# Mixture-of-experts tail of a language-model tower: results scattered into rows of their own and summed per batch, instead of accumulated by the DMA

## What is computed

```
h = tok(x)                              # per token: 6-qubit circuit on 36 angles -> 6 numbers -> 192 features
h = h + attention(layernorm(h))         # single head, width 192, per batch
h = h + moe(layernorm(h))               # 8 experts, top 2, gelu MLP 192 -> 384 -> 192
def moe(x):
    scores = x @ Wg;  s, idx = top_k(scores, 2);  p = softmax(s)
    y_e = gelu(x @ W1[e] + b1[e]) @ W2[e] + b2[e]
    return p[0] * y[idx[0]] + p[1] * y[idx[1]]
```

## Time and profile before

| | us |
|---|---|
| median of 3 runs | 389.87 (388.54 to 391.79) |
| profiled execution: span from first to last instruction | 338.6 |
| time of that execution outside the span | not given by the page; against the median 51.3 |
| POOL busy | 250.2 |
| PE busy | 240.9 |
| DVE busy | 177.6 |
| ACT busy | 95.2 |

### The profile page before, as it was taken

The page is one execution under the profiler, slowest core; times in us unless marked ns, Lnnn a source line. Parts: engine busy times, 40 slices in busy tenths (PEclk is TensorE's granted clock), DMA queues, the critical chain, the costliest instruction groups (busy, mean ns, idle before and its releaser), DMA issues. The chain is left out here.

```text
span 338.6 us, 6221 instructions
## 1 busy us (share of the span) xinstructions
PE 240.9 (71%) x1585; PEld 162.0 (48%) x1585; DVE 177.6 (52%) x698; ACT 95.2 (28%) x223; POOL 250.2 (74%) x283
## 2 busy tenths in 40 slices
PE   0831973668478989768654899999999587999500
PEld 0621641223243445444421678777777365877400
DVE  5758997488998866684699322232222122122200
ACT  1002001354324144634233323332432132133000
POOL 5778979309968777766777388888883888888673
PEclk9999995558955556965555599999999799699955
DMA  6710019900000001111123146656461556564510
GB/s 191 201 13 11 0 45 400 382 5 2 2 0 9 12 13 60 63 57 60 59 70 103 22 54 69 64 62 67 53 69 18 60 62 65 61 69 50 59 10 0
DMA packets 28141, 22.61 MB, mean 67 GB/s; under 512 B 15434, under 2 KB 25546, under 8 KB 27787
## 3 DMA queue, kind: packets, MB, share of 16 engines
q0 software_dynamic: 13296, 7.95, 21.1%
q1 hardware_dynamic: 14524, 14.23, 13.0%
q10 hardware_dynamic: 288, 0.03, 0.1%
HBM read 7.25 MB, written 15.63 MB: 68 GB/s over the span
## 5 line engine op out<-in xcount | busy, mean ns | idle before, releaser
L709 POOL DMA_INDIRECT out<-up x71 | 110.3, 1554 | 33.1 <-issue 13.9
L1972 PE MATMUL bank_b<-down,up 128*128 x426 | 91.2, 354 | 5.0 <-DVE up L1473 1.0
L1972 PEld LDWEIGHTS bank_b<-down,up 128*128 128x128 f32 x426 | 72.9, 200 | 22.6 <-issue 18.8
L1473 DVE TENSOR_SCALAR up<-bank_b,up 128x192 f32<-128x192 f32 x71 | 29.6, 418 | 97.5 <-PE bank_b L1972 84.9
L657 POOL DMA_INDIRECT routed<-rows,slot x64 | 61.9, 968 | 23.9 <-issue 18.0
L472 POOL DMA_INDIRECT theta_all<-angles,ids x32 | 32.4, 1012 | 10.9 <-issue 9.0
L1651 ACT ACTIVATE up<-bank_a 128x384 f32<-128x384 f32 x71 | 31.3, 497 | 3.4 <-PE bank_a L1962 2.9
L1775 PE MATMUL bank_b<-queries_t,keys_t 32*128 32x512 f32 x64 | 26.1, 900 | 6.9 <-ACT keys_t L1499 3.4
L1782 PE MATMUL bank_a<-keys_t,wt 32*128 32x512 f32 x64 | 27.6, 949 | 3.8 <-DVE nmax L1133 2.1
L1663 ACT COPY up<-bank_c 128x384 f32<-128x384 f32 x18 | 8.6, 478 | 61.8 <-PE bank_c L1951 58.7
L1133 DVE TENSOR_REDUCE nmax<-bank_a 128x2 f32<-128x1024 f32 x16 | 19.5, 1219 | 11.5 <-PE bank_a L1782 11.3
(11 more groups left out here) (420 smaller groups left out, 369.4 us busy)
## 6 DMA issues: line engine op xcount, KB each, us to landing
routed<-pad_rows SPq DMA_DIRECT2D x8, 528.0 KB, 5.7
out<-hres SPq DMA_DIRECT2D x8, 384.0 KB, 2.4
down<-down_w SPq DMA_DIRECT2D x1, 2304.0 KB, 11.9
up<-up_w SPq DMA_DIRECT2D x1, 1536.0 KB
out<-up POOLq DMA_INDIRECT x71, 3.5
up<-routed SPq DMA_DIRECT2D x69, 16.0 KB
routed<-rows,slot POOLq DMA_INDIRECT x64
up<-up_w SPq DMA_DIRECT2D x1, 780.0 KB
```

The costliest lines, as they stand in the source:

```text
L709: pool.indirect_dma_start(out=out_rows, out_offset=bass.IndirectOffsetOnAxis(xb[:, m // STEP % RING, m % STEP, DEST:DEST + 1].bitcast(I32) ...
L1473: dve.tensor_scalar(y[:, m % RESULTS, :], bank_b[:, m % 2, 0:D], xb[:, m // STEP % RING, m % STEP, SHARE:SHARE + 1], None, ALU.mult).then_ ...
L1972: mm = pe.matmul(bank_b[:, m % 2, 0:D], hid[:, m % STEP, c * P:(c + 1) * P], down[:, bass.ds(first + c * D, D)], start=(c == 0), stop=(c = ...
```

## The change

- GpSimd scatters the results without add, into a DRAM tensor `results` of 8192 rows, one for each token and choice (`DEST` now counts to 2 x TOKENS). The waits on shared blocks, their arithmetic and the early stores of `hres` are gone. The bounds check stays.
- Each batch's two result rows per token are read back (`load_results`) and VectorE adds both to `hres` (`add_results`), then the batch is stored. Batches 0 to 5 are summed inside the loop at blocks fixed in `SUM_AT`, 6 and 7 after it. SyncE reads batch b back when the blocks that can hold its rows have landed.
- The order of the blocks no longer goes by expert alone. The first EARLY = 25 are whole blocks of the first four batches, worked out by `early_table` on VectorE once these are routed, ahead of batch 4's `variance2`. The rest come in groups by batch (what four batches leave whole, then what batches 4, 5, 6, 7 complete), worked out by `late_table`, spread over partitions by one matmul (`late_columns`) and written by `late_numbers`. Within a group they go by expert. 24 blocks are loaded without waiting for the last four batches' rows; the first 16 as soon as four batches are scattered.
- `pick_up` and its copy for steps 0 and 1, and the first `block_transpose`, move into the last attention iterations; ScalarE's GELU table is loaded ahead of the last `a2t_copy`.
- The readback of the last batch waits until the last block with real rows has landed (`need`); blocks after it are padding.

```diff
     RING = 4
-    SEEN = BATCHES - 2
     RESULTS = 8
+    EARLY_BATCHES = CHUNK_BATCHES[0]
+    EARLY = 2 * EARLY_BATCHES * SEQ // P - (E - 1)
+    EARLY_STEPS = EARLY // STEP
+    LATE = BLOCKS - EARLY
+    GROUPS = 2 + BATCHES - EARLY_BATCHES
...
+    results = nc.dram_tensor("results", (2 * TOKENS, D), F32, kind="Internal").ap()
...
+    results_view = results.rearrange("(k b p j) d -> b p k (j d)", k=2, b=BATCHES, j=TILES)
...
+        def whole_after(b):
+
+            return 2 * SEQ * (max(b + 1, EARLY_BATCHES)) // P + E - 2
+
+        def picked_in(s):
+
+            return bank_b[:, s, 0:HID] if s < 2 else bank_c[:, 0:HID]
+
+        SUM_AT = (46, 48, 53, 55, 59, 62)
+        STORE_AT = (45, 47, 51, 53, 57, 60)
...
+            def load_block(m):
+                row = sp.value_load(t_i[0:1, 0, m:m + 1], min_val=0, max_val=ROWS - P)
                 sp.dma_start(xb[:, m // STEP % RING, m % STEP, :], routed[bass.ds(row, P), :]
                              ).then_inc(block_in[m // STEP % RING], 16)
...
+            def load_results(b):
+                sp.dma_start(results_in[b % 2], results_view[b]).then_inc(results_back[b % 2], 16)
+
+            def store(b):
+                sp.wait_ge(summed, b + 1)
+                sp.dma_start(out_view[b], hres[:, b, :]).then_inc(out_done, 16)
+
             sp.wait_ge(table_done, 1)
-            first_rows = [block_row(m) for m in range(0, STEP, 2)]
-            sp.wait_ge(scattered, 16 * (2 * TILES * SEEN - 1))
-            rows_written(0)
-            sp.sem_inc(first_ready, 1)
-            for m, row in zip(range(0, STEP, 2), first_rows):
-                load_block(m, row)
-            for r in range(1, RING):
-                rows_written(r)
-                for m in blocks_of(r):
-                    load_block(m, block_row(m))
-            sp.wait_ge(scattered_last, 16 + 16 * 2 * TILES * (BATCHES - SEEN))
-            for m in range(BLOCKS):
+            sp.wait_ge(scattered_early, 16 * 2 * TILES * EARLY_BATCHES)
+            for m in range(RING * STEP):
+                load_block(m)
+            for m in range(LEAST - 1):
                 sp.wait_ge(added[m % RESULTS], 16 * (m // RESULTS) + 16)
-                sp.sem_inc(landed, 1)
-                if m + RING * STEP < BLOCKS:
-                    load_block(m + RING * STEP, block_row(m + RING * STEP))
-            sp.wait_ge(h2_out, 16 * BATCHES)
+                following = m + RING * STEP
+                if following == EARLY_STEPS * STEP:
+                    sp.wait_ge(table_done, 2)
+                    sp.wait_ge(scattered_late, 16 * 2 * TILES * (BATCHES - EARLY_BATCHES))
+                if following < BLOCKS:
+                    load_block(following)
+                if m == whole_after(0):
+                    load_results(0)
+                    load_results(1)
+                for b in range(BATCHES - 2):
+                    if m == STORE_AT[b]:
+                        store(b)
+                        if b < 3:
+                            load_results(b + 2)
+                for b in (5, 6):
+                    if m == whole_after(b):
+                        load_results(b)
+            last = sp.value_load(need[0:1, 0:1], min_val=1, max_val=BLOCKS - LEAST + 1)
+            sp.wait_ge(landed, last)
+            hold(sp)
+            load_results(BATCHES - 1)
+            store(BATCHES - 2)
+            store(BATCHES - 1)
+            sp.wait_ge(out_done, 16 * BATCHES)
...
-            pool.wait_ge(h2_out, 16 * BATCHES)
-            pool.wait_ge(order_done, 1)
             for m in range(BLOCKS):
-                last_shared = pool.value_load(t_i[0:1, 1, m:m + 1], min_val=1, max_val=BLOCKS + 1)
                 pool.wait_ge(y_done, m + 1)
-                pool.wait_ge(landed, last_shared)
-                hold(pool)
                 pool.indirect_dma_start(
-                    out=out_rows, out_offset=bass.IndirectOffsetOnAxis(
+                    out=results, out_offset=bass.IndirectOffsetOnAxis(
                         xb[:, m // STEP % RING, m % STEP, DEST:DEST + 1].bitcast(I32), 0),
-                    in_=y[:, m % RESULTS, :], in_offset=None, bounds_check=TOKENS - 1,
-                    oob_is_err=False, compute_op=ALU.add).then_inc(added[m % RESULTS], 16)
+                    in_=y[:, m % RESULTS, :], in_offset=None, bounds_check=2 * TOKENS - 1,
+                    oob_is_err=False).then_inc(added[m % RESULTS], 16)
...
+            def early_table():
+
+                step(dve.tensor_scalar(full_i[:, 1, :], full_i[:, 0, :], 7, None, ALU.arith_shift_right))
+                join()
+                step(dve.tensor_copy(full[:, :], full_i[:, 1, :]))
+                step(dve.tensor_copy(cum[:, 0, :], full_i[:, 1, :]))
...
+                step(dve.tensor_scalar(skip[:, :], full[:, :], -float(P), float(REGION), ALU.mult, ALU.add))
+                c = prefix(cum, E, (1, 2, 4))
+                step(dve.tensor_tensor(ge[:, :, :], blk[:, 0:EARLY].unsqueeze(1).to_broadcast([P, E - 1, EARLY]),
+                                       cum[:, c, 0:E - 1].unsqueeze(2).to_broadcast([P, E - 1, EARLY]), ALU.is_ge))
+                join()
+                step(dve.tensor_reduce(t_exp[:, :], ge.rearrange("p e m -> p m e"), AX.X, ALU.add))
+                step(dve.tensor_tensor(ge_w[:, :, :], ge, skip[:, 0:E - 1].unsqueeze(2).to_broadcast([P, E - 1, EARLY]),
                                        ALU.mult))
...
+                join()
+                step(dve.tensor_reduce(t_skip[:, :], ge_w.rearrange("p e m -> p m e"), AX.X, ALU.add))
+                step(dve.tensor_scalar(t_own[:, 0:EARLY, 0], t_exp[:, :], own[:, 0:1], None, ALU.is_equal))
+                step(dve.tensor_scalar(t_i[:, 1, 0:EARLY], t_exp[:, :], float(HC * D), None, ALU.mult))
+                join()
+                dve.scalar_tensor_tensor(t_i[:, 0, 0:EARLY], blk[:, 0:EARLY], float(P), t_skip[:, :], ALU.mult, ALU.add
+                                         ).then_inc(table_done, 1)
...
+            def late_table():
+
+                counted = bank_c[:, COUNT_AT:COUNT_AT + (GROUPS - 1) * E].rearrange("p (g e) -> p g e", e=E)
+                step(dve.tensor_scalar(count_i[:, 1:GROUPS], counted, float(P - 1), None, ALU.add))
+                step(dve.tensor_copy(count_i[:, 0], counted[:, 0]))
...
+                h = prefix(run_end, RUNS, (1, 2, 4, 8, 16, 32))
+                end = run_end[:, h, :]
+                step(dve.tensor_tensor(run_n[:, :], run_n[:, :], end, ALU.subtract))
+                step(dve.tensor_scalar(run_ge[:, :], end[:, 0:RUNS - 1], pos[:, 0:1], None, ALU.is_le))
+                step(dve.tensor_scalar(need[:, :], end[:, RUNS - 1:RUNS], -float(LEAST - 1), None, ALU.add))
...
+                step(dve.tensor_reduce(late[:, 0:2], run_w[:, :, :], AX.X, ALU.add))
+                join()
+                step(dve.tensor_tensor(late[:, 2:3], late[:, 1:2], pos[:, :], ALU.add))
+                step(dve.tensor_scalar(late_diag[:, 0, :], ident[:, 0:LATE], late[:, 0:1], None, ALU.mult))
+                join()
+                dve.tensor_scalar(late_diag[:, 1, :], ident[:, 0:LATE], late[:, 2:3], None, ALU.mult
+                                  ).then_inc(late_ready, 1)
...
+            def late_numbers():
+
+                dve.wait_ge(late_spread, 1)
+                step(dve.tensor_scalar(t_own[:, EARLY:BLOCKS, 0], bank_c[:, 0:LATE], own[:, 0:1], None,
+                                       ALU.is_equal))
+                step(dve.tensor_scalar(t_i[:, 1, EARLY:BLOCKS], bank_c[:, 0:LATE], float(HC * D), None,
+                                       ALU.mult))
+                join()
+                dve.tensor_scalar(t_i[:, 0, EARLY:BLOCKS], bank_c[:, LATE:2 * LATE], float(P), None,
+                                  ALU.mult).then_inc(table_done, 1)
...
+            early_table()
+            expert_of(0)
+            expert_of(1)
+
             for i in range(LAST[0] + 2, BATCHES + 2):
...
+            late_table()
+            late_numbers()
+
+            def add_results(b, k):
+
+                if b == 0 and k == 0:
+                    dve.wait_ge(h2_copied, 2 * BATCHES)
+                if k == 0:
+                    dve.wait_ge(results_back[b % 2], 16 * (b // 2) + 16)
+                else:
+                    join()
+                last = dve.tensor_tensor(hres[:, b, :], hres[:, b, :], results_in[b % 2][:, k, :], ALU.add)
+                if k == 0:
+                    step(last)
+                else:
+                    last.then_inc(summed, 1)
...
                 weighted(m)
                 if m % STEP == 1 and m // STEP + 2 < STEPS:
                     expert_of(m // STEP + 2)
+                for b in range(BATCHES - 2):
+                    if m in (SUM_AT[b], SUM_AT[b] + 1):
+                        add_results(b, m - SUM_AT[b])
+            for b in (BATCHES - 2, BATCHES - 1):
+                add_results(b, 0)
+                add_results(b, 1)
...
```

(36 more changed lines are left out.)

294 lines of the change are left out of this document (114 added, 180 removed).

## The result

The changed kernel took 370.23 us (median of 4, 367.62 to 374.9) against 390.03 us for the kernel before (388.54 to 391.79): a ratio of 0.9484, 95% interval 0.9424 to 0.9545, 19.8 us faster. The forecast was 367.0, range 360 to 378.

A forecast was written before the change was run, and what follows sets the result against it. POOL's accumulating result scatters (1.855 us a block against TensorE's 1.625) and ordering waits were taken as the bound. Start -0.2, loop 12.0 and tail 11.3 gave 23.1 us off 389.87: 367, range 360 to 378.

The forecast's parts named there:

- The scatter: Result scatter on POOL without add: 0.96 us instead of 1.55, period 1.26 us against TensorE's 1.625 per block.
- The estimate by the Trainium skill: Plain result scatter priced by descriptors, two instead of three with the add: 1.55 x 2/3 = 1.03 us.
- The start of the loop: First up projection of the expert loop at 188.6 against 188.42 before; head start and early table cancel: -0.2 us.
- The early table: On VectorE ahead of variance2(4): 4.2 us, no cover, moving the rest of the attention stage by as much.
- the picks and the transpose: Steps 0 and 1 prepared on TensorE ahead of residual(5, 0): 3.7 us, less 1.4 of idle, 2.3 showing.
- The loop: Expert stage, up projections 6.50 us apart, adds hidden: first up projection to last result 118.3 us instead of 130.3, 12.0 gained.
- The tail: From the last result to the end, with last readback, sums and store: 8.6 us instead of 19.9, 11.3 gained.
- the final output waits for block 65: End of kernel: blocks 66 to 70 are padding; scatter 65 ends at 301.1, the span at 315.5, 14.4 us later.
- 51.3 us lie around it, unchanged: Profiled span set against the median time: 51.3 us outside the span, kept, so 389.87 - 23.1 = 366.8.
- POOL stays the bound: Rival: row length or bounds check makes the scatter's 1.55 us, only the waits go: 382 us; chance 0.15.
- the readback's stall of the loop: Rival: VectorE waits for readbacks in the expert loop, decisive from 8.2 us each, 408 us at 15; chance 0.05.
- the two rivals on the start: Early table costs more, start 4 to 5 us later: 372, chance 0.09; little felt, 5 us earlier: 362, chance 0.10.

The follow-up runs named there:

- a2: Kernel before with only the add taken out of the result scatters, waits on shared blocks kept: 317.12 us against 338.64, ratio 0.9359, lower level.
- c1: Kernel before, unedited, profiled again: 339.05 us, span 337.2, lower level.
- c3: Changed kernel, unedited, run again at the lower level: 316.58 us, span 315.7, ratio 0.9336 to the kernel before.
- c2: Kernel before with only the add taken out of the result scatters, a second time: 317.32 us against 339.07, ratio 0.9406, lower level.
- b3: Changed kernel without the eight readbacks and with adds of a single column: 366.89 us beside 367.0 for the changed kernel, upper level.
- d2: Changed kernel without the eight readbacks and with adds of a single column, a second time: 363.75 us, ratio 0.9669 to the kernel before, upper level.
- jobs a and b: Two of the later measuring jobs; the kernel before took 338.64 us in the first of them (lower level), 385.63 us in the second (upper).
- b4: Changed kernel with the add put back into the result scatters, rows zeroed by one DMA: 373.63 us beside 367.0 for the changed kernel, upper level.
- b1: Changed kernel, unedited, run again at the upper level: 367.0 us, span 365.4, ratio 0.9455 to the kernel before.
- d3: Changed kernel with the add put back into the result scatters, a second time: 370.42 us, ratio 0.9945 to the kernel before, upper level.

## Why the forecast was right, step by step

**The scatter.** 0.96 us forecast, 0.98 measured (median; 1.00 on the mean), period 1.29. The choice to price it by the nearest plain indirect DMAs of 128 indices was right, and a2 shows that neither row length nor bounds check is in the 1.55. The estimate by the Trainium skill ("Collectives: The Full Stack", section "The bandwidth ceiling: the fold count and why AG ≠ RS ≠ AR"), 1.03 us, is close too, but that rule is one for ring transfers between cores, and its count is not what the queue shows: with the add a scatter has 96 packets more, beside some 39 for an average DMA of this queue without it (6480 in 167).

**The start of the loop.** The early table took 4.05 us on VectorE's path (4.2 forecast), variance2(4) came at 144.29 (145 forecast), the picks and the transpose 3.19 us (3.64 forecast, the rows at half clock). Between c1 and c3 variance2(4) moves from 139.96 to 144.29 and the last residual copy from 179.1 to 184.2, 5.1 us (7.7 forecast); the first up projection comes right behind it and not 7.8 us later, as in c1. It is at 184.78 against 188.6 forecast and 186.94 in c1. But the old order of work without the add has it at 184.81 (c2) and 186.07 (a2), and before at 188.42, 187.66 and 186.94. Over these five traces of one order it moves by 3.6 us, and the one trace of the new order lies at their early end. So price and gain of the head start cancel to within some 4 us, and no finer; the forecast's -0.2 us and a gain of 2 or 3 us both fit. A small slip in the recorded sum: routed scatters that shift by 4.2 us end at 190.15 + 4.2 = 194.35 and not 194.1. They ended at 193.24.

**The loop.** 130.4 us from the first up projection to the end of the last result in c1, 119.5 in c3: 10.9 bought, 12.0 forecast. TensorE's pace is (296.74 - 191.42) / 16 = 6.58 us a step where 6.50 was taken: that is the missing 1.3 us. Where it comes from is not shown. c2 has neither adds nor readbacks and is no shorter, but it keeps the ordering waits, and its steps are even (6.60 us over the first nine, 6.54 over the last seven) where c3's grow from 6.52 to 6.66 in the stretch that holds the readbacks.

**The tail.** 19.9 us before, 11.5 after: 8.4 bought, 11.3 forecast. This is the term that was mis-sized most, by 2.9 us. Held against my own chain, c3 shows where they lie. The last result ends 4.6 us behind the end of scatter 65 and not 5.8 (1.2 of the 2.9). The reason is a queue on POOL that I had not allowed for: result 65 is ready at 297.26, its scatter starts behind those of blocks 63 and 64 at 298.65, and the scatter of block 63 had itself waited 1.9 us for its result, which VectorE made after the first wide add of batch 5 and 1.6 us of waiting for that batch's readback.

```profile
294.00 0.96 DVE L1521 TENSOR_TENSOR hres<-hres,keys_t 128x768 f32<-128x768 f32 x1 [1.57 <-DMA keys_t<-results]
...
296.84 0.42 DVE L1531 TENSOR_SCALAR up<-bank_b,up 128x192 f32<-128x192 f32 x1 [0.36 <-PE bank_b L1957]
```

From the scatter's end to the issue of the last readback at 304.21 it is 4.6 us, not 4.0 (0.6); the readback takes 4.6, not 4.3 (0.3); batch 7 is summed at 310.79, 2.0 us later and not 1.9 (0.1); from there to the end it is 4.9, not 4.2 (0.7).

I had also written "the final output waits for block 65" and followed that chain alone. What I left out is POOL: it has five padding scatters to go and 8.7 us behind the last. In c3 that is worth no more than some 0.2 us beyond the chain, by the estimate above; it decides as soon as the chain gets shorter, as in b3 and d2. Before, the end lies 4.9 to 5.0 us behind the last scatter, and I carried it on as the 1.5 us behind a landing.

**The sum.** Start, loop and tail between c1 and c3: 2.2 + 10.9 + 8.4 = 21.5 us of span, and 22.5 in the medians, against 23.1 forecast. The start bought 2.4 us more than forecast (2.2 against -0.2), loop and tail 1.1 and 2.9 less. That the sum is so close is in part luck: the late start of my forecast and its short tail offset each other.

**The absolute number.** 367.0 came from a premise that failed: "51.3 us lie around it, unchanged". Only 1.7 us lie around the span; the trace and the times beside it belonged to different levels. That the number held all the same was luck: the first result was taken at the upper level too, and that level adds about the same to either kernel: at the upper one the changed kernel has 41.5 us more ahead of the first up projection (226.26 against 184.78) and 8.4 us more in the loop (127.9 against 119.5). By the right premise the forecast is 315.5 + 1.7 = 317.2 at the lower level; measured 316.58. That it was 3 us low at the upper one fits the loop, where the plain kernel's steps take 7.2 us and the add's 7.42 cost little; it is not shown without a trace of before there.

**The rivals.** "POOL stays the bound" fell with 0.98 us; the readback's stall of the loop did not come (in c3 VectorE waited 5.8 us for the eight readbacks, 2.7 of them for the last); the two rivals on the start lie within what one order of work moves by itself.

## What to carry to other kernels

Set a profiled span against the time of that same execution; if the page does not give it, a gap of 50 us to the median is a finding to be explained and not an overhead to be carried along. When a scatter accumulates, price the add first: here, at the lower level, one word of the instruction was worth the 22 us, and the tables, readbacks and sums around it only kept the result right without it, at no cost. When a chain at the end is shortened, list every engine that is still running behind it, its padding work included.

## What the runs showed of the chip that I had not expected

- An accumulating indirect scatter of 128 rows of 768 bytes keeps GpSimd busy for 1.55 us, a plain one for 0.98, and has 96 packets more on the queue.
- The whole program runs at one of two levels, 336 to 341 or 370 to 392 us for the same kernel, job by job, once each on the same chip (jobs a and b). At the upper level TensorE's products are seen late by the engines that wait for them: up to 8 us late, in five places of the attention stage, some 0.7 us a step in the loop of the kernels with the plain scatter, and not with the add (6.50 us in b4), while the granted clock of TensorE is 1.00 in the loop as at the lower level. In the attention stage it is lower with the pauses (0.55 from 130 to 150 us in the first job's trace, 0.76 in c3); which is cause and which effect the rows do not say. POOL's instructions keep their length (a result scatter 1003 ns in b1, 1002 in c3). What it is stays open, and so does whether the kernel before shows the same waits there, since all three of its traces are of the lower level.
- GpSimd's program ends 8.7 us after its last plain scatter in the changed kernel, 7.4 us in the no-add kernel (308.28 to 315.7 in a2), and 4.9 to 5.0 us in the kernel before, with the DMA engines idle for most of that time. With the add put back it is 5.6 us in b4 and 6.6 in d3. I have no cause for it. A loop that ends with the last real block was not tried.
